# Another order of the four matmul phases of a batch in a split-precision batched matmul with GELU

## What is computed

```python
z1 = jnp.einsum('bfi,bir->bfr', x, v[:, 0]) / inch
z = jnp.einsum('bfr,bor->bfo', z1, u[:, 0]) / r
y = jnp.einsum('bfi,oi->bfo', x, W) + fc_bias + z + b
return jax.nn.gelu(y, approximate=False)
# and outside: x = x + that
```

## Time and profile before

| | |
|---|---|
| time, median of 3 runs | 398.92 us (398.77 to 401.34) |
| the profiled execution | 398.59 us, of which its span is 396.8 us |
| PE busy | 384.8 us, 97% of the span, 3065 matmuls |
| PEld busy | 305.0 us (77%) |
| DVE busy | 294.2 us (74%) |
| ACT busy | 201.2 us (51%) |
| DMA | mean 216 GB/s |
| granted clock of TensorE | 1.0 |

### The profile page before, as it was taken

How to read it: one execution, slowest core, us unless ns; L and a number is a source line. 1 busy time by engine, 2 the same in 40 slices (tenths; PEclk the granted TensorE clock), 3 DMA queues, 4 the chain that set the end, 5 groups by cost and what they waited for, 6 DMA issues and landing times.

```text
span 396.8 us, 7835 instructions
## 1 busy us (share of the span) xinstructions
PE 384.8 (97%) x3065; PEld 305.0 (77%) x3065; DVE 294.2 (74%) x188; ACT 201.2 (51%) x214; POOL 0.7 (0%) x5
## 2 busy tenths in 40 slices
PE   8998999999999999999999999999999999999995
PEld 3676888777877777877777787777787777788874
DVE  3579787777797777798777788777779777779852
ACT  3367246654446664445665444665444666444542
POOL 0000000000000000000000000000000000000000
PEclk9999999999999999999999999999999999999999
DMA  7778888887667877666877666777666787766123
GB/s 195 219 177 268 256 247 235 269 263 239 197 207 211 264 209 245 212 197 214 247 211 251 217 194 220 228 229 238 235 192 216 212 254 217 241 199 201 72 115 133
DMA packets 27756, 85.75 MB, mean 216 GB/s; under 512 B 6832, under 2 KB 6960, under 8 KB 23776
## 3 DMA queue, kind: packets, MB, share of 16 engines
q1 hardware_dynamic: 27088, 84.41, 69.2%
q10 hardware_dynamic: 656, 1.18, 1.0%
HBM read 35.75 MB, written 33.55 MB: 175 GB/s over the span
## 4 chain that ended last, share of the span: by engine, by line
PE 68%; ACT 17%; SPq 5%; issue 4%; DMA 4%; DVE 1%; ACTq 1%; DVEq 0%
PE y L413 65%; ACT w_high L244 12%; SPq L175 5%; ACT result L290 4%; DMA f_stack<-f_parts 2%; DMA base_w<-w_t 1%; PE y L405 1%; DVE w_low L305 1%; PE y L401 1%; PE y L397 1%; PE update L482 1%; ACTq L290 1%; SPq L161 0%; ACTq L284 0%; SPq L189 0%
## 5 line engine op out<-in xcount | busy, mean ns | idle before, releaser
L413 PE MATMUL y<-x_high,w_high 64*128 64x512 f32 x928 | 185.3, 394 | 3.9 <-ACT result L290 2.4
L413 PE MATMUL y<-x_low,w_high 64*128 64x512 f32 x928 | 182.5, 387 | 0.0
L290 ACT ACTIVATE result<-y,bias 128x512 f32<-128x512 f32 x128 | 81.0, 687 | 174.5 <-PE y L413 166.1
L305 DVE TENSOR_TENSOR w_low<-full_w,w_high 128x2048 fp32r<-128x2048 f32 (+1 forms) x38 | 74.3, 1955 | 79.5 <-ACT w_high L244 79.1
L413 PE MATMUL y<-x_high,w_low 64*128 64x512 f32 x928 | 124.7, 387 | 0.0
L413 PEld LDWEIGHTS y<-x_high,w_high 64*128 64x128 f32 x928 | 88.2, 184 | 32.0 <-ACT result L290 13.5
L413 PEld LDWEIGHTS y<-x_high,w_low 64*128 64x128 f32 x928 | 88.2, 185 | 17.4
L413 PEld LDWEIGHTS y<-x_low,w_high 64*128 64x128 f32 x928 | 88.5, 185 | 16.3
L348 DVE TENSOR_TENSOR result<-result,x_in 128x1024 f32<-128x1024 f32 (+1 forms) x65 | 78.0, 1201 | 6.0 <-ACT result L290 6.0
L309 DVE SCALAR_TENSOR_TENSOR full_w<-update,base_w 128x2048 f32<-128x2048 f32 (+1 forms) x38 | 74.0, 1947 | 9.0 <-DMA base_w<-w_t 6.7
L305 DVE TENSOR_TENSOR x_low<-x_in,x_high 128x2048 fp32r<-128x2048 f32 (+1 forms) x38 | 74.0, 1946 | 5.0 <-ACT x_high L253 5.0
(11 more groups left out here) (15 smaller groups left out, 29.7 us busy)
## 6 DMA issues: line engine op xcount, KB each, us to landing
out_t<-result SPq DMA_DIRECT2D x63, 512.0 KB, 3.4
x_in<-x_t SPq DMA_DIRECT2D x31, 1024.0 KB, 6.3
f_stack<-f_parts SPq DMA_DIRECT2D x186, 64.0 KB, 4.0
f_stack<-f_parts SPq DMA_DIRECT2D x124, 32.0 KB, 3.8
x_in<-x_t ACTq DMA_DIRECT2D x4, 256.0 KB, 9.1
base_w<-w_t SPq DMA_DIRECT2D x4, 256.0 KB, 8.1
f_parts<-factors SPq DMA_DIRECT2D x1, 896.0 KB, 7.1
out_t<-result SPq DMA_DIRECT2D x2, 256.0 KB, 2.5
```

The source lines that it names most:

```text
L290: nc.scalar.activation(result[j % SLOTS][:, m, :], y[m][:, :], ACT.Gelu, bias=bias[:, bass.ds(b * CHUNKS + m, 1)]).then_inc(gelu_ready, 1)
L305: nc.vector.tensor_tensor(out, whole, high.bitcast(fp32), ALU.subtract).then_inc(ready, 1)
L413: return nc.tensor.matmul(y[m][:, :], w[rows, c, m * P:(m + 1) * P], x[rows, c, :], start=first, stop=last)
```

## The change

The second and the third phase change places, and the test whether a phase opens is changed with them (before: phases 0 and 1; now: phases 0 and 2). Nothing else differs: the same matmuls run with the same operands, and the thresholds of all waits for a pair of tiles are the same numbers.

```diff
-    PHASES = ((0, 1), (2, 3), (1, 0), (3, 2))
+    PHASES = ((0, 1), (1, 0), (2, 3), (3, 2))
...
                 tiles = PHASES[phase]
-                opens = phase < CHUNKS // TILES
+                opens = phase % TILES == 0
                 if opens:
```

## The result

The changed kernel takes 409.89 us (median of 4 runs, 409.44 to 410.73) where the kernel before takes 398.85 (four runs, one more than in the table above). The ratio is 1.0267, with a 95% interval of 1.0229 to 1.0305. So it is 11.0 us slower; the forecast was 407.5 us, in a range of 404 to 411. In a second comparison it took 407.97 us against 399.26, ratio 1.0227 (1.0171 to 1.0283), 8.7 us slower.

What follows compares the result with a forecast made beforehand. TensorE, 97% busy, was taken as the bound, with a wait at A for ACT's Gelus and w_high copy. From 398.6 us, 21.5 added less 12.7 removed (+8.8) gave 407.5 us; 80% range 404 to 411.

Steps and rivals of the forecast that it cites:

- What is removed: TensorE's late start at each batch's first phase, behind Gelu and the w_high copy, goes: 12.7 us gained.
- A: A batch's phases by tiles: A (0, 1), B (1, 0), C (2, 3), D (3, 2); order A C B D becomes A B C D.
- The 0.64 us of the last batch: Last batch's late entry: delays of 0.10, 0.10, 0.31 and 0.13 us at its first and w_low matmuls, all expected to go.
- What is added: TensorE waits for its own sums (half_summed) at B and D, two in each of 29 batches: 58 x 0.37 = 21.5 us.
- gate: One wait of TensorE for its own last result, at the start of B or D: 0.37 us, bounds 0.34 to 0.40.
- the handover: From a phase's last pair to the closing phase's first pair: 0.48 us instead of 0.227, 0.25 lost.
- the restart: After the wait, the closing phase's second pair comes 0.34 us after its first instead of 0.23: 0.11 lost.
- The handover's price: At B and D, the Trainium skill's increment tail (87 ns for two) would add 0.04 us each, about 2 us in all.
- The first (only the emptying is paid, 0.16 us): Rival at B and D: only emptying the array is paid, 9.3 us in all; not slower, 395.2 us; 5%.
- The second (no restart cost): Rival at B and D: handover costs 0.25 us, restart nothing; about the same, 400.4 us; 5%.
- The third (a wait on itself takes longer): Rival at B and D: TensorE's wait on itself takes 0.10 us longer, 0.47 a gate; 413.2 us; 5%.
- The fourth (another wait at A): Rival: w_high, x_low or the rank update's DMAs arrive last, so the wait at A stays; 420 us; 5%.

Runs made afterwards that it cites:

- neither wait: Changed kernel, closing phases keeping each tile on its array half (half the contraction left out, the other summed twice), waits for half_summed removed: 386.41 us, ratio 0.967.
- the early copy: Kernel before, in its old order of phases, with the next batch's w_high copied ahead of Gelu 0 instead of behind it: 385.27 us, ratio 0.9653.
- the control with the early copy: Changed kernel with the next batch's w_high copied ahead of Gelu 0: 407.83 us, ratio 1.0217.

## Why the prediction was right, and where a size was off

**The time.** 409.89 us lies in the range, 2.4 us above the forecast; the repetition, 407.97, is 0.5 above it.

**What is removed.** Right in mechanism: A starts 0.22 us behind the rank update's last pair, and no engine took the wait over. ACT's part came as laid out: the batch whose next rank update starts at 163.19 began 12.11 us earlier, at 151.08, and its Gelu 0 starts at 157.69, 6.6 us in. The term was 12.7 us. The batch with no wait is 11.333 us, not the 11.36 that I read off batch 2, so the wait was worth 11.790 - 11.333 = 0.457 us, 28 x 0.457 = 12.8 us.

The 0.64 us of the last batch, "and all of it goes", did not all go. After the change:

```profile
392.31 1.07 PE L413 MATMUL y<-x_high,w_low 64*128 64x512 f32 x8
...
393.31 0.19 PEld L397 LDWEIGHTS y<-x_high,w_high 128*128 128x128 f32 x1 [0.35 <-issue]
393.31 0.50 PE L397 MATMUL y<-x_high,w_high 128*128 128x512 f32 x1
393.64 0.40 PE L401 MATMUL y<-x_low,w_high 128*128 128x512 f32 x1
...
395.27 1.08 PE L405 MATMUL y<-x_high,w_low 128*128 128x512 f32 x4
```

The first matmul still comes 0.32 us behind the last pair of D (392.31 + 3 x 0.227 = 392.99), and the second 0.33 behind it, as in the earlier trace rows; with neither wait, and with the early copy, it is the same. So these two losses of 0.10 were not the wait for w_high. They stand where TensorE goes over from half to full matmuls; their cause is open. Only the other 0.44 went, which were the wait for w_low. The whole gain is 12.8 + 0.44 = 13.2 us, and the kernel with neither wait has it: 12.4 in the steady stretch and 0.9 behind it.

**What is added.** 0.37 us a gate was forecast, 0.387 measured: 0.25 for the handover and 0.11 for the restart, as put together from the rows of before, and 0.026 for the pairs behind it (B takes 2.857 us, of which 0.111 is the second pair's delay), where I allowed 0.01. 58 x 0.387 = 22.4 us instead of 21.5.

**The sum.** 22.4 - 13.2 = +9.2 us, against +8.8. The added term was 0.9 us too small and the removed one 0.5; that they partly cancel was luck. The repeated pair shows 8.7 (between medians) and 405.6 - 396.1 = 9.5 (between spans), of which 0.3 is a later start of batch 2 (38.63 against 38.33). The first comparison shows 11.0. The profiled pair there differs by 12.1 us of span: 27 x 0.317 = 8.6 in the steady stretch, 0.7 for the two gates of batch 2, 1.6 for its 3.4 us at the lower clock (8 steps of 0.43 instead of 0.23), and 1.3 because batch 2 started at 40.39 instead of 39.07, while the factors landed; the end gives 0.1 back. The 1.6 and the 1.3 are the start's. Runs of both orders have them or not, and the forecast had no term for them: it spoke of "run to run differences" and gave them some 1.6 us.

**The handover's price.** The sentence on the tail of increments ("TensorE: Matmul & The Clock Gate" of the Trainium skill, section "The cost: per-tile semaphore tail") would have made the gate 0.04 us dearer, 0.40 to 0.41. The 0.48 us handover shows no such tail beyond the 0.05 us already in the row of before.

**The rivals.** The first (only the emptying is paid, 0.16 us) falls with the rows at 154.51 and 154.84: the release and the restart are both there. So does the estimate from the Trainium skill ("TensorE: Matmul & The Clock Gate", section "Single matmul latency") that spoke for it: its 379 ns agrees with the 0.39 us drawn for a matmul here, whose end is modelled, but the gate holds the release and the restart besides. The second (no restart cost) falls with the 0.34 us step. The third (a wait on itself takes longer) does not show: 0.04 us from release to load, as behind Gelu. The fourth (another wait at A) is refuted by the steady stretch, whose batches of 12.107 us are 11.333 and two gates, and by the control with the early copy, which changes nothing.

## What to carry to other kernels

A wait of an engine for its own last result hardly shows in a busy share (96% here against 97%) and was cheap here only with work in between or beside another wait: place independent instructions, here a rank update of 0.45 us, between the producer and the wait, and 0.39 us shrinks to 0.03. Before reordering the bound engine to get rid of a wait, look at the releasing engine's queue: here one copy stood ahead of what was waited for though its input had been ready for 4.3 us, and moving it gave the whole gain with no gate. Price a wait at the place where it stands: the same kind of gate cost 13 us at one phase boundary and about 1 us at another.

## What was not expected of the hardware

In three profiled executions, of the changed kernel, of the kernel with neither wait and of the old order with the early copy, TensorE's clock was at its lower level for 3.4 us in batch 2 (pairs 0.43 us apart instead of 0.227), following an idle time of 2.4 to 3.2 us ahead of the rank update; with 2.65 us in another it was not. This and the landing of the first factors make a spread of some 3 us at the start of the program, and made up about 2 of the first measured 11.0 us; two rows, the start of batch 2 and its length, tell it apart from the change.

At two places with two waits a gate's handover was dearer in some batches, 0.57 to 0.58 us instead of 0.48: at C in 23 of 29 batches, at D only in the five outside of the loop. The number of waits does not tell the two apart, the place in the loop does in part, and the cause is open.
